# Broadcasting attention scores in a graph-attention layer: plain float32 matmuls, or fp32r matmuls of a rounded part and a remainder

## The reference

```python
h = einsum('bnd,ade->bane', x, W);  th = tanh(h)
attn_src = einsum('bane,aeo->bano', th, w_src)
attn_dst = einsum('bane,aeo->bano', th, w_dst)
attn = leaky_relu(attn_src + swapaxes(attn_dst, 2, 3), 0.2)
attn = softmax(where(~adj, -999, attn))
f = elu(einsum('banm,bame->bane', attn, h) + b)
gate = sigmoid(x @ H_w.T + H_b)
x = layernorm(x + gate * f + (1 - gate) * x)
```

## Time and profile before

| | before |
|---|---|
| three runs, us | 3290.34, 3291.20, 3293.18; median 3291.2 |
| span of the profiled execution, us | 3285.7 (no time around the span is shown) |
| TensorE matmul busy | 3071.5 us, 93% |
| VectorE busy | 1692.9 us, 52% |
| ScalarE busy | 1407.6 us, 43% |
| GpSimd busy | 843.8 us, 26% |
| L546, the broadcast, busy | 99.5 us in 256 records |
| L292, the diagonal, busy | 94.4 us in 64 instructions |

### The profile page before, as it was taken

The page is one execution under the profiler, slowest core; times in us unless marked ns, Lnnn a source line. Parts: engine busy times, 40 slices in busy tenths (PEclk is TensorE's granted clock), DMA queues, the critical chain, the costliest instruction groups (busy, mean ns, idle before and its releaser), DMA issues.

```text
span 3285.7 us, 55951 instructions
## 1 busy us (share of the span) xinstructions
PE 3071.5 (93%) x20800; PEld 2970.4 (90%) x20800; DVE 1692.9 (52%) x3820; ACT 1407.6 (43%) x4261; POOL 843.8 (26%) x457
## 2 busy tenths in 40 slices
PE   6999999999999994699999999999999999999998
PEld 6888888888888883699999999999999999999998
DVE  4777777777777775342343433433423334334334
ACT  4677666766676665322322323223223223232232
POOL 2555655565556554000000000000000000000000
PEclk9999999999999996799999999999999999999999
DMA  2111111111111112201010010010010100100100
GB/s 97 40 39 39 44 43 39 39 44 43 39 39 44 44 39 71 94 24 36 21 40 20 21 40 20 21 40 20 25 35 20 40 21 20 40 21 21 39 20 20
DMA packets 60261, 120.07 MB, mean 37 GB/s; under 512 B 22208, under 2 KB 22208, under 8 KB 60096
## 3 DMA queue, kind: packets, MB, share of 16 engines
q1 hardware_dynamic: 60096, 117.50, 10.5%
HBM read 67.15 MB, written 50.33 MB: 36 GB/s over the span
## 4 chain that ended last, share of the span: by engine, by line
PE 54%; DVE 2%; ACT 2%; DMA 1%; issue 1%; SPq 0%; DVEq 0%; ACTq 0%
PE L_ps_k L117 13%; PE L_ps_q L117 13%; PE L_ps_a L117 12%; PE L_ps_a L954 10%; PE L_ps_s L917 3%; PE L_ps_c L937 2%; ACT L_probs L723 1%; DVE L_cT_lo L812 1%; ACT L_cT_hi L709 1%; DVE L_logits L788 1%; PE L_ps_q L871 0%; PE L_ps_s L871 0%; PE L_ps_k L871 0%; PE L_ps_pt L924 0%; DVE L_neg_max L794 0%
## 5 line engine op out<-in xcount | busy, mean ns | idle before, releaser
L681 POOL TENSOR_TENSOR L_x_tok<-L_x_tok,L_bf_all 128x768 f32<-128x768 f32 x64 | 116.5, 1840 | 1793.3 <-PE L_ps_s L871 1793.3
L788 DVE SCALAR_TENSOR_TENSOR L_logits<-L_ps_s,L_mask 64x256 f32<-64x256 f32 x192 | 81.0, 422 | 804.3 <-PE L_ps_s L917 801.3
L117 PE MATMUL L_ps_k<-L_xT_hi,L_w_hi 128*128 128x256 f32 x1152 | 331.1, 287 | 0.0
L117 PE MATMUL L_ps_q<-L_xT_hi,L_w_hi 128*128 128x256 f32 x1152 | 328.5, 285 | 0.0
L117 PE MATMUL L_ps_k<-L_xT_hi,L_w_lo 128*128 128x256 f32 x1152 | 326.0, 283 | 0.0
L117 PE MATMUL L_ps_q<-L_xT_hi,L_w_lo 128*128 128x256 f32 x1152 | 326.0, 283 | 0.0
L117 PE MATMUL L_ps_k<-L_xT_lo,L_w_hi 128*128 128x256 f32 x1152 | 325.9, 283 | 0.0
L117 PE MATMUL L_ps_q<-L_xT_lo,L_w_hi 128*128 128x256 f32 x1152 | 325.9, 283 | 0.0
L745 ACT COPY L_v_tok<-L_ps_a 128x384 f32<-128x384 f32 x128 | 61.3, 479 | 556.8 <-PE L_ps_a L117 556.8
L323 ACT ACTIVATE L_probs<-L_logits,L_neg_max 128x64 f32<-128x64 f32 x768 | 256.2, 336 | 94.5 <-DVE L_neg_max L446 94.5
L117 PE MATMUL L_ps_h<-L_w_hi,L_xT_hi 128*128 128x384 f32 x768 | 271.2, 353 | 21.2 <-DVE L_w_lo L106 21.2
(11 more groups left out here) (119 smaller groups left out, 8156.3 us busy)
## 6 DMA issues: line engine op xcount, KB each, us to landing
L_x_tok<-x SPq DMA_DIRECT2D x64, 384.0 KB, 2.8
x_scratch<-L_x_out SPq DMA_DIRECT2D x64, 384.0 KB, 2.3
L_x_tok<-x_scratch SPq DMA_DIRECT2D x32, 768.0 KB, 4.2
out<-L_x_tok SPq DMA_DIRECT2D x32, 768.0 KB, 3.4
L_stage<-W SPq DMA_DIRECT2D x6, 384.0 KB, 5.2
L_stage<-H_t SPq DMA_DIRECT2D x6, 384.0 KB, 4.0
L_x_tok<-Wq SPq DMA_DIRECT2D x6, 384.0 KB, 3.6
L_x_tok<-Wk SPq DMA_DIRECT2D x6, 384.0 KB, 3.7
```

The costliest lines, as they stand in the source:

```text
L117: ins = pe.matmul(out, left[a][c], right[b][c], start=(n == 0), stop=(n == len(terms) - 1))
L681: pool.tensor_tensor(x_tok[:, s, t], x_tok[:, s, t], bf_all[:, :], ALU.add).then_inc(biased, 1)
L788: dve.scalar_tensor_tensor(out=logits[r].rearrange("p (h t) m -> p h t m", t=GT), in0=ps_s[r, :].rearrange("p (h t m) -> p h t m", h=2, t= ...
```

## The change

`dst` (128x12) is split on VectorE into a part rounded to fp32r and the remainder. POOL makes a diagonal of each, in fp32r, so one multiplication becomes two. TensorE broadcasts both with `same_graph` in fp32r and adds them up in `ps_pt`: two matmuls for each half. `same_graph` is now an fp32r copy of a block matrix made in float32.

```diff
-        dst_diag = sb("dst_diag", [P, D])
+        dst_split = sb("dst_split", [P, 2, HEADS0], F32R)
+        dst_diag = sb("dst_diag", [P, 2, D], F32R)
...
-        same_graph = sb("same_graph", [P, P])
+        graph_block = sb("graph_block", [P, P])
+        same_graph = sb("same_graph", [P, P], F32R)
...
 # POOL
-                    pool.wait_ge(dst_done, T + 1)
+                    pool.wait_ge(dst_lo_done, T + 1)
                     if has(-1):
                         pool.wait_ge(bc_done, T)
-                    pool.tensor_tensor(
-                        per_head(dst_diag[:, :], HEADS0), over(dst[:, :], HEADS0, NODES),
-                        node_of[:, :].unsqueeze(1).to_broadcast([P, HEADS0, NODES]), ALU.mult).then_inc(diag_done, 1)
+                    for part in range(2):
+                        pool.tensor_tensor(
+                            per_head(dst_diag[:, part, :], HEADS0), over(dst_split[:, part, :].bitcast(F32), HEADS0, NODES),
+                            node_of[:, :].unsqueeze(1).to_broadcast([P, HEADS0, NODES]),
+                            ALU.mult).then_inc(diag_done, 1)
...
 # VectorE, once, before the steps
+            dve.wait_ge(graph_ok, 4)
+            dve.tensor_copy(same_graph[:, :], graph_block[:, :]).then_inc(graph_ok, 1)
...
 # VectorE, in each step
-                        dve.wait_ge(diag_done, T)
+                        dve.wait_ge(diag_done, 2 * T)
                     dve.tensor_reduce(dst[:, :], per_head(th_dst[:, :], HEADS0), AX_X, ALU.add).then_inc(dst_done, 1)
+                    dve.wait_ge(dst_done, T + 1)
+                    dve.tensor_copy(dst_split[:, 0, :], dst[:, :]).then_inc(dst_hi_done, 1)
+                    dve.wait_ge(dst_hi_done, T + 1)
+                    dve.tensor_tensor(dst_split[:, 1, :], dst[:, :], dst_split[:, 0, :].bitcast(F32),
+                                      ALU.subtract).then_inc(dst_lo_done, 1)
...
 # TensorE
-                    pe.wait_ge(diag_done, T + 1)
+                    pe.wait_ge(diag_done, 2 * (T + 1))
                     for s in range(2):
-                        ins = pe.matmul(ps_pt[:, s, 0:HALF], same_graph[:, :],
-                                        dst_diag[:, s * HALF:(s + 1) * HALF], start=True, stop=True)
+                        for part in range(2):
+                            ins = pe.matmul(ps_pt[:, s, 0:HALF], same_graph[:, :],
+                                            dst_diag[:, part, s * HALF:(s + 1) * HALF],
+                                            start=(part == 0), stop=(part == 1))
                     ins.then_inc(bc_done, 1)
```

More of the change, by code:

```diff
@@ L200, in layer0 @@
         tanh_done, h_copied, mask_done = sem("tanh_done"), sem("h_copied"), sem("mask_done")
-        thdst_done, thsrc_done, dst_done, src_done, diag_done = (
-            sem(n) for n in ("thdst_done", "thsrc_done", "dst_done", "src_done", "diag_done"))
+        thdst_done, thsrc_done, dst_done, dst_hi_done, dst_lo_done, src_done, diag_done = (
+            sem(n) for n in ("thdst_done", "thsrc_done", "dst_done", "dst_hi_done", "dst_lo_done", "src_done",
+                             "diag_done"))
         sum_done, leaky_done, masked_done, max_done, exp_done = (
@@ L271, in _ @@
             identity(pool, ident[:, :], ones[:, :], memsets, ident_ok)
-            pool.wait_ge(graph_ok, 6)
+            pool.wait_ge(graph_ok, 7)
             pool.wait_ge(consts_in, 64)
@@ L397, in _ @@
             dve.memset(probsT[:, :, :], 0.0).then_inc(bd_zero, 1)
-            dve.memset(same_graph[:, :], 0.0).then_inc(graph_ok, 1)
+            dve.memset(graph_block[:, :], 0.0).then_inc(graph_ok, 1)
             dve.wait_ge(graph_ok, 1)
             for g in range(2):
-                dve.memset(same_graph[g * NODES:(g + 1) * NODES, g * NODES:(g + 1) * NODES], 1.0).then_inc(graph_ok, 1)
+                dve.memset(graph_block[g * NODES:(g + 1) * NODES, g * NODES:(g + 1) * NODES], 1.0).then_inc(graph_ok, 1)
             dve.memset(masked[:, :], MASKED0).then_inc(graph_ok, 1)
+            dve.wait_ge(graph_ok, 4)
+            dve.tensor_copy(same_graph[:, :], graph_block[:, :]).then_inc(graph_ok, 1)
             dve.wait_ge(ident_ok, 1)
@@ L499, in _ @@
             pe.wait_ge(ident_ok, 1)
-            pe.wait_ge(graph_ok, 3)
+            pe.wait_ge(graph_ok, 5)
             def transpose_x(T, u):
```

## The result

The changed kernel takes 3362.4 us (3360.8 to 3362.7) against 3291.5, a ratio of 1.0217 (95% interval 1.0205 to 1.0229): 71 us slower. The forecast was 3369 us, in a range of 3330 to 3405.

The account below looks back on a forecast made before the run. The prediction took a layer-0 ring of VectorE and ScalarE, 19.32 us per step, as the bound. Span 3285.7, plus 62 x 1.25 = 77.5, 0 for TensorE and setup, and 5.5 from span to median: 3369 us, range 3330 to 3405.

Parts of the forecast that it names:

- The ring without TensorE: Layer 0 step: 12.01 us VectorE, 7.25 ScalarE, two handovers of 0.03 make 19.32 us; TensorE is in none of it.
- The hold of L463: VectorE's L463 waits for the end of POOL's second multiplication, finishing 1.13 to 1.67 us later; 1.25 taken per step.
- The sign that the prediction named for it: In the profile after, VectorE's L463 at about 1.9 to 2.1 us in place of 0.96.
- The order: Whether L463 finds POOL's second multiplication running (early case) or the first still running and gets in between (late cases).
- The other order: L463 between POOL's two multiplications is hardly late; the second ends near 619.55, L297 starts 1.45 later, L492 1.35 later.
- The copy: VectorE's 128x12 copy before L459: may wait for POOL's L287, about evenly; if so, 0.31 more, step 1.44 to 1.67 longer.
- the free-running case: If the copy does not wait for POOL, copy and subtraction are done by 615.30 to 615.53, L287 ending at 615.22.
- the 0.14 that a held instruction saves: L436 on VectorE saves 0.14 of its 0.96 us behind a wait for POOL; the forecast applied this to the subtraction.
- TensorE's gain: L546's broadcast: 0.60 us less per step, 38 us in all, counted as 0; rival that it arrives: 3253 us, chance 0.05.
- The sum: Layer 0: 62 steps x 1.25 = 77.5 us, plus span 3285.7 and 5.5 from span to median: 3368.7 us.
- Rounding on POOL: POOL's diagonal multiplications at L292: rounding the output to fp32r costs nothing, so the second takes 1.48 us as well.
- A condition that was wrong: Layer 0: the forecast is wrong if the granted clock falls below 1.00 in TensorE's longer waits, which were not priced.

Follow-up runs that it names:

- the late bias: POOL starts the bias only when VectorE has done the tile's mask; on the kernel before: 3232.8 us, 0.9826; on the changed kernel: 3305.2 us, 1.0050.
- the late second multiplication: The changed kernel, with POOL waiting for L475 before the second multiplication, nothing else; 3369.1 us, 1.0240.
- the kernel with L475 first and four gates: The changed kernel, with POOL waiting for L475 before the second multiplication and four gate buffers in place of two; 3251.6 us, 0.9885.

## Why the prediction was right

*The ring without TensorE* was right in the main, and shown: 58 us could be taken out of layer 0 without touching a matmul (the late bias), and 38 us of matmul time taken out of TensorE gave 5.

*The hold of L463* was right in place and kind. The forecast was 1.13 to 1.67 us, measured were 1.26; the 0.82 by which L436 outlasts POOL came back to the hundredth. The sign that the prediction named for it, L463 at 1.9 to 2.1 us, doesn't follow from its own sum: 0.96 and 1.13 to 1.67 are 2.09 to 2.63, and 2.23 was measured.

*The order* was the first of the two forecast: the second multiplication is already running when L475 is released. The other order, with L475 in between, came only when POOL was told to wait, and then its price appeared at L504 nearly as worked out (1.29 against 1.35).

*The copy.* The forecast left open whether it waits for POOL, and charged 0.31 if it does. It does wait: it starts 0.54 to 0.70 before the end of L290 and takes 0.58 to 0.72 accordingly, and its record always ends 0.02 to 0.04 after POOL's (628.30 and 628.27 in the step shown). The Trainium skill says that a float32 copy from SBUF to SBUF runs in a two-port mode and so shuts GpSimd out (SBUF — State Buffer, "SBUF: two separate sides"); the trace agrees in that the copy waits for POOL, in all 64 steps. But little is charged for it: the subtraction is done at 628.51, 0.24 after L290's end, inside the 0.08 to 0.31 of the free-running case, and the 3387 us worked out for a copy that waits is too high. The prediction took the 0.14 that a held instruction saves off the subtraction. It belongs to the copy, the one that is held: were its own length the subtraction's 0.17, it would end 0.03 after POOL (an estimate), as it does.

*TensorE's gain* was taken as 0, since L420 was read as starting behind L417 alone. That reading was wrong for most steps: L420 waited for the product in 48 of 62, if only for 0.06 to 0.10 in most of them. The gain was 5.2 us. That it lies under the 5.6 given as the most is luck, as that bound took the 0.09 of one step for all, and 15 steps gained 0.14 or more.

*The sum* came out 6.3 us too high. The 5.2 of TensorE were left out, and the 5.5 carried from span to median were 3.3 in the changed kernel (3362.4 - 3359.1), whose profiled execution lay nearer to its median. The other way go 0.6 for the hold, 1.25 taken for 1.26, and 1.1 for the later start of the first step. The last 0.6 stays open.

*Rounding on POOL* is free: 1474 ns against 1475.

*A condition that was wrong*: the prediction was to fail if the granted clock in layer 0 fell below 1.00 in the longer waits. It did fall (0.98 from 36 to 1263, 1.00 in the earlier trace rows), and nothing came of it (below).

*What it overlooked*: L436 served as evidence for the exclusion, but its own 0.88 us per step were taken as given. They were the larger gain to be had, 58 us for one wait.

## What to carry to other kernels

Where VectorE and GpSimd run side by side, look up each VectorE instruction with two SBUF operands on the path that sets the step, and ask which GpSimd instruction is running when it becomes ready; a record that is longer by the rest of the other engine's instruction, with no wait for that engine listed before it, is the sign. An operand in PSUM, or letting the instruction that is not urgent wait for the urgent one, removed the hold here. Then look where the one that waits ends up: the late bias left all of its 58 us, the late second multiplication came back as 1.29 us at L504. And a matmul saved is worth only what the ring lets through: here 5 us of 38.

## What the runs showed of the hardware

A held VectorE instruction shows as a long one: L475 takes 2.23 us, and the only wait listed before it is the one for ScalarE (0.71, against 0.82 in the earlier trace rows). A list of waits does not find the hold.

A copy of 128x12 from SBUF to SBUF on VectorE is held by POOL's multiplication (0.60 us mean, against 0.17 for the subtraction behind it, which found POOL free). The predicated copy is not: L448 takes 1.09 us on average behind L283, and in the kernel with L475 first and four gates (L450 there) it takes 1.09 from 626.84 on, in the midst of L283's 625.81 to 628.44.

The granted clock fell in 19 of the 64 steps of the changed kernel. In windows of six us, 216 to 222 and 236 to 242, the column before the DMA share (the third from the end) gives its mean:

```profile
216.00:222.00 6.00, 5.07 (x22) 5.08 (x23) 5.22 (x7) 5.91 (x16) 4.79 (x4) 0.72 0.00 0
236.00:242.00 6.00, 4.33 (x26) 3.95 (x26) 5.08 (x6) 5.91 (x18) 4.96 (x3) 1.00 0.00 0
```

TensorE had waited 2.42 us before the first and 1.37 before the second:

```profile
216.93 1.42 PE L548 MATMUL L_ps_pt<-L_ident,L_probs 128*128 128x128 f32 x6 [2.42 <-ACT L_probs L328]
...
218.46 0.52 PE L117 MATMUL L_ps_g<-L_w_lo,L_xT_hi 128*128 128x384 f32 x1
218.78 0.52 PE L117 MATMUL L_ps_g<-L_w_hi,L_xT_lo 128*128 128x384 f32 x1
...
237.43 0.88 PE L548 MATMUL L_ps_pt<-L_ident,L_probs 128*128 128x128 f32 x6 [1.37 <-ACT L_probs L328]
```

The projections behind the longer wait start 0.32 apart in place of 0.18; from 218.0 to 220.3 the granted clock is 0.50, the lower of the two levels (1.2 in place of 2.4 GHz). A wait of 2.41 us was followed by no fall in the step shown first, so its length alone does not decide. The step takes no harm: from L475 to L427 it is 226.71 - 219.35 = 7.36 us in the step with the fall and 247.19 - 239.87 = 7.32 in the other. From 93 to 463 the clock fell in every second step and from 504 to 997 in none, and a step takes 20.5 us in both stretches. TensorE had that much time to spare.

```profile
219.35 2.23 DVE L475 SCALAR_TENSOR_TENSOR L_feat<-L_att,L_feat 128x768 f32<-128x768 f32 x1 [0.71 <-ACT L_feat L367]
226.71 0.96 DVE L427 TENSOR_TENSOR L_att<-L_ps_xa,L_row_inv 128x768 f32<-128x768 f32 x1
239.87 2.21 DVE L475 SCALAR_TENSOR_TENSOR L_feat<-L_att,L_feat 128x768 f32<-128x768 f32 x1 [0.72 <-ACT L_feat L367]
247.19 0.96 DVE L427 TENSOR_TENSOR L_att<-L_ps_xa,L_row_inv 128x768 f32<-128x768 f32 x1
```
